# Second layer's maximum products paired with its own scores, and its value products in one block, in a two-layer vision tower

## The reference

```python
h = x @ W_tok + positions                         # 29 -> 128
h = h + attn0(group_norm(layernorm(h)))           # 8 heads of 64, softmax over 1024 keys
h = h + ffn0(layernorm(h))                        # two 128 x 128 products, gelu between
h = h + attn1(layernorm(h))                       # 8 heads of 16, softmax over 1024 keys
h = h + switch(layernorm(h))                      # 16 experts of 128 x 128, top one, capacity 1.2
```

## Time and profile before

| what | value |
|---|---|
| median of 3 runs | 8374.74 us (8361.47 to 8421.3) |
| the profiled execution, its own time | 8371.84 us |
| its span, first to last instruction | 8370.1 us |
| mean granted TensorE clock | 0.833 |
| TensorE busy | 7405.4 us, 88% |
| VectorE busy | 5002.4 us, 60% |
| ScalarE busy | 3213.9 us, 38% |
| GpSimd busy | 1774.3 us, 21% |

### The profile page before, as it was taken

How to read it: one execution, slowest core, us unless ns; L and a number is a source line. 1 busy time by engine, 2 the same in 40 slices (tenths; PEclk the granted TensorE clock), 3 DMA queues, 4 the chain that set the end, 5 groups by cost and what they waited for, 6 DMA issues and landing times.

```text
span 8370.1 us, 124378 instructions
## 1 busy us (share of the span) xinstructions
PE 7405.4 (88%) x39399; PEld 4297.5 (51%) x39399; DVE 5002.4 (60%) x11545; ACT 3213.9 (38%) x6291; POOL 1774.3 (21%) x1623
## 2 busy tenths in 40 slices
PE   6798998989989899898988989899898998989987
PEld 4555555545545455454555545555554555545532
DVE  5664665656666565565656656566565665656554
ACT  3343443433434343343433434334343443434431
POOL 2322222222222222222221222222222221222200
PEclk8887897988988878798887888879788787888866
DMA  2220211111121110211102111111111111111000
GB/s 63 47 47 20 49 32 40 39 43 36 26 49 39 33 39 23 49 39 33 39 22 52 37 43 39 29 43 29 43 39 41 31 32 43 38 40 39 22 24 7
DMA packets 89184, 308.91 MB, mean 37 GB/s; under 512 B 23942, under 2 KB 30022, under 8 KB 78278
## 3 DMA queue, kind: packets, MB, share of 16 engines
q1 hardware_dynamic: 88518, 300.53, 15.6%
HBM read 49.33 MB, written 41.94 MB: 11 GB/s over the span
## 4 chain that ended last, share of the span: by engine, by line
issue 63%; POOL 17%; PE 14%; DVE 4%; DMA 1%; POOLq 0%; SPq 0%; ACT 0%; DVEq 0%; ACTq 0%
POOL pr_lo L456 9%; POOL on L1183 3%; PE bank L776 3%; PE bank L749 2%; POOL on L1175 2%; PE bank L735 2%; PE bank L792 1%; PE bank L806 1%; PE bank L793 1%; PE bank L774 1%; DVE hm L1448 1%; DMA stacks<-parts 1%; DVE mxh L1458 1%; POOL h L1153 1%; PE bank L816 1%
## 5 line engine op out<-in xcount | busy, mean ns | idle before, releaser
L1458 DVE TENSOR_REDUCE mxh<-bank 128x1 f32<-128x512 f32 x4096 | 2761.3, 689 | 2300.8 <-PE bank L749 2275.4
L1029 ACT ACTIVATE pr<-bank 128x512 f32<-128x512 f32 x4096 | 2400.1, 598 | 3343.0 <-PE bank L776 3276.2
L749 PE MATMUL bank<-stacks 128*128 128x512 f32 (+1 forms) x4096 | 2036.1, 508 | 403.3 <-DVE mxh L1458 369.6
L776 PE MATMUL bank<-stacks 65*128 65x512 f32 (+1 forms) x4096 | 1929.2, 482 | 5.7 <-ACT pr L1029 5.7
L749 PEld LDWEIGHTS bank<-stacks 128*128 128x128 f32 (+1 forms) x4096 | 862.8, 214 | 1088.0 <-DVE mxh L1458 791.0
L456 POOL TENSOR_TENSOR pr_lo<-pr 128x1024 bf16<-128x1024 f32 x496 | 940.1, 1895 | 1933.7 <-ACT pr L1029 1933.7
L792 PE MATMUL bank<-v,pr 128*128 128x129 bf16 x8192 | 1308.1, 251 | 7.5 <-DVE pr_lo L456 5.1
L793 PE MATMUL bank<-v,pr_lo 128*128 128x129 bf16 x7936 | 1272.2, 251 | 0.0
L776 PEld LDWEIGHTS bank<-stacks 65*128 65x128 f32 (+1 forms) x4096 | 839.5, 210 | 767.7 <-issue 609.6
L774 PE MATMUL bank<-stacks 128*128 128x512 f32 x2048 | 1049.8, 513 | 47.0 <-issue 40.8
L792 PEld LDWEIGHTS bank<-v,pr 128*128 128x128 bf16 x8192 | 904.1, 113 | 357.1 <-issue 338.7
(11 more groups left out here) (180 smaller groups left out, 5209.8 us busy)
## 6 DMA issues: line engine op xcount, KB each, us to landing
stacks<-parts SPq DMA_DIRECT2D x384, 512.0 KB, 6.7
parts_d<-pr SPq DMA_DIRECT2D x16, 2048.0 KB, 6.5
stacks<-parts_d SPq DMA_DIRECT2D x224, 128.0 KB
stacks<-parts_d SPq DMA_DIRECT2D x224, 64.0 KB
stacks<-mrow SPq DMA_DIRECT2D x512, 2.0 KB
out<-hm SPq DMA_DIRECT2D x16, 512.0 KB, 2.7
stacks<-pr SPq DMA_DIRECT2D x32, 128.0 KB
stacks<-pr SPq DMA_DIRECT2D x32, 64.0 KB
```

The costliest lines, as they stand in the source:

```text
L749: mm(maxb[k % 2][:, :], qs[:, t * P:(t + 1) * P], ks[:, g * HALF:(g + 1) * HALF], start=True, stop=True).then_inc(max_filled.sem, 1)
L776: mm(bank[:, :], k_stack(layer, head)[0:last, kk], q_stack(layer, head)[0:last, q], start=(layer == 1), stop=True).then_inc(score_filled.s ...
L1029: act.activation(pr[:, at % 2, kt, :], score[k % 2][:, :], ACT.Exp, scale=SCALES[layer]).then_inc(exp_done.sem, 1)
L1458: dve.tensor_reduce(mxh[:, layer, n // 2, n % 2:n % 2 + 1], maxb[k % 2][:, :], AX_X, ALU.max)\
```

## The change

In the segments that hold both layers, every maximum tile moves two steps later, so that the tiles of a layer stand in the eight steps of that layer's own units. The rows follow two steps later too. The tiles made early in the serial part are 16, no longer 18. The value products of a layer-1 unit (eight key blocks) stand together at step 3. Projections stand one step earlier. The expert groups, before at steps 2 and 3 of twelve layer-1 units and four layer-0 units with VectorE's part at step 4, stand at steps 5 and 6 of nine layer-1 units (7, 11, 13, 15, 19, 21, 23, 27, 29) and seven layer-0 units (12, 14, 20, 22, 24, 26, 28), with VectorE's part at step 7.

```diff
--- before.py
+++ after.py
@@ -41,13 +41,14 @@
 
     if kind not in BOTH:
         return n - 12
+
     if layer == 0:
-        return n - 18 if n < 8 else n - 10
-    return n - 10 if n < 8 else n - 2
+        return n - 16 if n < 8 else n - 8
+    return n - 8 if n < 8 else n
 
 
 def row_step(kind, layer, g):
-    return (((-8, 8), (0, 16))[layer] if kind in BOTH else (-4, 4))[g]
+    return (((-6, 10), (2, 18))[layer] if kind in BOTH else (-4, 4))[g]
 
 
 def stack_step(kind, layer, head):
@@ -129,7 +130,7 @@
         return {}
     if kind == "first":
         return {f"{w}{c}.{g}": 32 * (c - 1) + 7 + n for c in range(1, 4) for n, (w, g) in enumerate(PROJECTS)}
-    return {f"{w}{c}.{g}": 64 * c - 59 + 4 * n for c in range(1, 4) for n, (w, g) in enumerate(PROJECTS)}
+    return {f"{w}{c}.{g}": 64 * c - 60 + 4 * n for c in range(1, 4) for n, (w, g) in enumerate(PROJECTS)}
 
 
 def turn_slots(kind):
@@ -151,7 +152,7 @@
     else:
         at = {"ln": 2, "z": 6, "zT3.0": 10, "zT3.1": 11, "logits": 18, "route": 20, "rank": 26, "place": 33,
               "wT0": 42, "wT1": 43, "eb0": 46, "eb1": 47}
-        first = [8 * m + 2 for m in sorted([*range(7, 31, 2), 14, 18, 22, 26])]
+        first = [8 * m + 5 for m in (7, 11, 12, 13, 14, 15, 19, 20, 21, 22, 23, 24, 26, 27, 28, 29)]
     return {**at, **{f"e{n}.{d}": s + d for n, s in enumerate(first) for d in range(2)}}
 
 
@@ -794,19 +795,17 @@
                 if j % 2 == 1:
                     last.then_inc(o_filled.sem, 1)
 
-            def values1(seg, at, j):
+            def values1(seg, at):
                 _, u = units_of(seg.kind)[at]
                 n = o_place(seg.kind, 1, u)
-                te.wait_ge(exp_done.sem, exp_done.at(seg, 8 * at + 4 * j + 4))
-                if j == 0:
-                    te.wait_ge(o_drained.sem, o_drained.at(seg, n - 1))
+                te.wait_ge(exp_done.sem, exp_done.at(seg, 8 * at + 8))
+                te.wait_ge(o_drained.sem, o_drained.at(seg, n - 1))
                 col = (D1 + 1) * (u // 2)
-                for r in range(4):
-                    kt = 4 * j + r
+                for kt in range(T):
+                    r = kt % 4
                     last = mm(obank[n % 2][QUAD * r:QUAD * (r + 1), :], v1[:, kt, col:col + QUAD], pr[:, at % 2, kt, :],
-                              start=(j == 0), stop=(j == 1))
-                if j == 1:
-                    last.then_inc(o_filled.sem, 1)
+                              start=(kt < 4), stop=(kt >= 4))
+                last.then_inc(o_filled.sem, 1)
 
             def fold1(seg, at):
                 _, u = units_of(seg.kind)[at]
@@ -820,8 +819,8 @@
             def values(seg, at, j):
                 if units_of(seg.kind)[at][0] == 0:
                     values0(seg, at, j)
-                elif j < 2:
-                    values1(seg, at, j)
+                elif j == 1:
+                    values1(seg, at)
                 elif j == 3:
                     fold1(seg, at)
```

## The result

The changed kernel takes 9045.01 us, the median of four runs (9037.75 to 9046.74). The kernel before, beside it on the same chip, takes 8382.42 us (8361.47 to 8421.3, four runs). The ratio is 1.078, 95% interval 1.074 to 1.082: 7.8% slower. The prediction said 3.3% slower and 8400 to 8890 us. The direction was right, the size was not, and the time lies above the range.

A forecast was written before the change was run, and what follows sets the result against it. TensorE, busy 88% of the span, was taken to set the time. Savings of 25.9 and costs of 35.1 us a repetition gave +95 in all (8467 us); the clock's +190 made 8657, said as 8655, range 8400 to 8890.

The forecast's parts named there:

- the expert groups decide: TensorE stands behind VectorE's 2.15 us of expert instructions: +15.1 us a repetition in seven layer-0 units, +16.0 at eight layer-1 units.
- the small terms: Value block -3.7 us, projection waits -2.9, second-half score and tile 0.01 us apart; the repetition without experts gains 14.
- the pairs: Layer-1 steps 6 and 7, 48-row tiles beside 49-row scores: -6.9 us a repetition in second halves, -2.4 in first halves.
- The clock: Extra half-clock stretches, costing 1.7 us each, in first-half layer-1 units and layer-0 units: 13.6 x 14 = +190 us.
- (a): First-half layer-1 units without projection (13, 21, 25, 29) stay low one stretch longer: 1.7 x 4 = +6.8 us a repetition.
- (b): Half-clock stretch behind every second new 2.0 us stand in layer-0 units: 1.7 x 4 = +6.8 us a repetition (0 to 13.6).
- the rest of the sum: Terms besides expert stands and removed waits: value block -3.7, layer-0 steps -4.8, layer-1 steps -6.9 and -2.4, transpose +1.6, fold +2.4.
- rival 3: Layer-1 units at half clock nearly throughout, +380 us on 8467, layer-0 stretches +95 to +190: 8850 to 9040 us; chance 0.15.
- I take one, the nearer row having experts: Extra half-clock stretches per first-half layer-1 unit without projection: bounds none and two, one taken, 1.7 us each in four units.

The follow-up runs named there:

- the kernel with the old expert steps: The changed kernel with expert groups and projections both back at their old steps, leaving moved tiles and value block: 8305.6 us, 0.991 of the kernel before.
- the kernel with narrow `hm`: The changed kernel with the expert groups' vector instructions narrowed from 128 to 8 columns, all else in place: 8607.5 us, 1.028 of the kernel before.
- the first filled kernel: The kernel before plus one thrown-away 128 x 512 product per layer-1 unit, behind the tile of step 1: 8217.5 us, 0.981 of the kernel before.

## Why the prediction was right about the direction and wrong about the size

**Right: the expert groups decide, by stands.** The prediction had a stand of 1.5 to 2.2 us at step 2 of a layer-0 unit behind an expert group, and some 3.3 at a layer-1 entry behind one. The rows show 1.9 to 2.3 in eight layer-0 units and 3.5 to 3.95 in seven layer-1 units, in the units named. The waits were to go from 21.0 to about 45 us and went to 55.0. The list alone moves the kernel by +667 us, the rest alone, without the earlier projections, by -68 (8373.5 beside it, to 8305.6). That is shown.

**Right: the small terms.** Waits for the projection are gone. Score and tile start 0.01 us apart in the second half of a head. A value block of eight, at full clock, takes 1.86 us from its start to the next score, within the 1.8 to 2.0 named. The repetition without experts came out 21 us shorter where 14 was summed. The value block was to save 3.7 us a repetition and saved 4.4.

**Not kept: the pairs.** The prediction gave the 48-row tiles beside 49-row scores -6.9 and -2.4 us a repetition, and step 6 of the layer-0 units -4.8. Apart from the value block, the moved tiles save only in the repetition without experts (17 us); in those with experts they cost 1.6 us. One attention part of the kernel with the old expert steps shows it; it answers to the earlier trace rows:

```profile
3895.80:4313.30 417.50, 378.38 (x2198) 229.32 (x2197) 267.51 (x585) 177.98 (x356) 94.55 (x87) 0.87 0.14 31
```

TensorE is busy 16.2 us less than in the earlier trace rows, and the window is 2.1 us shorter: 14 us became idle time. Half of that is the wait for the row maximum, up from 21.0 us; most of the rest are waits for other VectorE work (3.3 us) and for ScalarE's probabilities (2.7 us), which the earlier trace rows doesn't have:

```profile
PE bank L750 <- DVE mxh L1457: 27.9, 26, 2.8
```

These terms were summed as if nothing waited behind them.

**Wrong: the price of the clock.** This is the step that failed, the one headed "The clock", in both of its terms. What half clock costs a unit is (1 - clock) x length, since at 0.50 half of the time is lost. The mean of the 14 repetitions, unit by unit:

| units | forecast, us | clock loss before | after | more |
|---|---|---|---|---|
| (a) first-half layer-1 units 13, 21, 25, 29 | +6.8 | 8.9 | 31.6 | +22.7 |
| (b) layer-0 units with a new stand (8, 12, 14, 16, 20, 22, 24, 28) | +6.8 | 0.0 | 11.5 | +11.5 |
| second-half layer-1 units (3, 7, 11, 15, 19, 23, 27, 31) | 0 | 27.5 | 29.6 | +2.1 |
| all others | 0 | 25.4 | 26.3 | +0.9 |
| a repetition | +13.6 | 61.8 | 99.0 | +37.2 |

- (a) took one extra stretch of 3.4 us in each of four first-half units. The clocks show some three extra in each. In unit 13 above, half clock holds 13.5 us where the prediction had one such stretch and one extra. Units 21, 25 and 29 went from 14.7, 15.4 and 13.8 us to 22.0, 21.2 and 21.9; this is not all clock, since some 2.6 us of each are the longer stand, but 3 to 6 us of each are more than the stand explains.
- (b) took half clock behind every second new stand in a layer-0 unit. It came behind 80 of 112, in units 8 and 28 always, in unit 14 once in 14.

From the two windows alone the loss is (1 - 0.86) x 419.6 = 59 us before and (1 - 0.80) x 468.0 = 94 after, 35 us a repetition more. (Some 3 and 5 us of these lie in the stands themselves.) The waits are the second, smaller miss: with both lines of each kernel they went from 23.9 to 56.5 us, +32.6, where 31.1 - 8.1 = 23.0 was summed. With the rest of the sum as it stood (-13.8: the pairs do save busy time, and what they lose again is in the waits) that makes 35 + 32.6 - 13.8 = 54 us a repetition; 52 were measured. Put into the forecast, the clock's 21 us a repetition add 298 us and the waits' 9.6 add 134. Against them stands the last segment, 35 us shorter, which I left out of the sum though the value block stands there too.

**Which case it was.** In the number it was rival 3, to which I gave 0.15: layer-1 units at half clock nearly throughout. Its 8850 to 9040 was summed wrongly: 8467 + 380 and its 95 to 190 for (b) make 8942 to 9037, so all of it lay above the range's end at 8890. The result is 8 us above that. But this is partly luck. Three quarters of rival 3's layer-1 price lay in six second-half units (20 us a repetition), and these did not get slower by the clock (+2.1 for all eight). The first-half units cost 22.7 us where rival 3 had 6.8. What spoke for a long low stretch in them was a row that the prediction had: 17.00 us at 0.50 with TensorE busy in all of it. The choice "I take one, the nearer row having experts" took the row of a unit in which expert products follow the first value blocks, and the change takes just those away.

**The cause.** For the layer-0 units it is the length of the stand: with 1.0 us instead of 2.0 behind unchanged products on TensorE, their clock loss is gone. For the first-half layer-1 units the place of full-precision products counts by itself: with the stands as they were, thrown-away products where the expert products had been took the clock loss of units 13, 21, 25 and 29 from 31.6 to 18.5 us a repetition, 13.1 of the 22.7 that the change had added, and made the kernel 136 us faster. Stands one us shorter left it at 32.3; in the second-half units they took it from 29.6 to 20.6. And a thrown-away product in a short stand pays: it makes the changed kernel 287 us faster and the kernel before 165. The page TensorE: Matmul & The Clock Gate of the Trainium skill (Why this matters for your kernels) asks for no long idle gap between bursts. The gaps behind which the clock fell here were short, 1.15 us before and 1.97 us after, and filling the short ones at layer-1 entries with work of no use paid.

**What stays open.** First-half units (score and tile on the same partitions, one after the other) lose the most to half clock, second-half units with the same stand much less; I have not shown why, nor why the clock holds in unit 14 behind a stand of 1.97 us and falls in others. The clock loss that the thrown-away products did not give back in first-half units (9.6 of 22.7 us) may be the longer stand's; no run shows it. How the 302 us between the kernel with narrow `hm` and the one with the old places (8607.5 and 8305.6) divide between the stands that are left and the place of the expert products is not measured. And the first filled kernel gained 165 us where I had expected 400: the stands of expert units took their part of it, by how much I can't tell.

## What to carry to other kernels

Work of a side engine that the bottleneck waits for belongs where the bottleneck has most of its own work in hand: here VectorE's 2.15 us made no wait in unit 13 beside two value blocks, and cost up to 2.8 us of TensorE standing between two units. Work that nobody waits for, the expert products, belongs in the stand: a list of steps that puts ten of the sixteen groups there took 4.5% off the kernel before, and one that puts them ahead of the stands added 8%. Where the granted clock is under 1 in a window, price a new stand by the time at half clock that can follow it, and take the longest row that the trace has of it for the range.

## What was not expected of the hardware

- Work added for nothing made the kernel faster: 240 products of 128 x 512 in the stands took 8382 to 8217 us, and in the changed kernel 9045 to 8758. In the repetition without experts the attention part went from 367.0 to 316.2 us, at a clock of 0.99.
- The clock stayed at half for 13.5 us at one stand, although TensorE was busy from the end of that stand on, with 59 matmuls, of 48 and 49 rows and of 129 columns among them. With one full-precision 128 x 512 product in each of the two steps ahead of the same place, and no stand left there, it was at 1.00 for the whole unit of 11.8 us.
- In units of this kind with the same stand, two thrown-away full-precision products behind the value products raised the clock from 0.60 to 0.65 up to 0.76 to 0.79.
- A stand of 1.97 us was followed by 3.3 us at half clock (stands of 1.9 to 2.3 us by a fall of the clock in 80 of 112 cases), one of 1.0 us in the same place by none.
